# Head of a four-layer graph network on one core: ScalarE normalizes x and copies h, the attention terms come out of h's own product, and two bodies of edge ranking move beside it

## The reference, cut to what matters

```
xn  = (x - mean(x)) / sqrt(var(x) + 1e-5)
h   = xn @ W_layer.T + b_layer
a1  = (h @ w_a1.T + b_a1)[:, 0]
a2  = (h @ w_a2.T + b_a2)[:, 0]
v   = leaky_relu(a1[row] + a2[col])        # softmax of v over the edges of a row
out = segment_sum(att[:, None] * h[col], row)
```

## Time and profile before

| | us |
|---|---|
| three runs | 6016.11, 6029.7, 6051.34 |
| median | 6029.7 |
| the profiled execution | 6056.04 |
| its span | 6054.2 |
| from the statistics of x to the ranking loop | 295.25 to 396.56 |
| POOL scatters bodies 4 to 32 | 289.52 to 1113.7 |
| POOL gathers h | 1113.7 to 2166.3 |

### The profile page before, as it was taken

The page is one execution under the profiler, slowest core; times in us unless marked ns, Lnnn a source line. Parts: engine busy times, 40 slices in busy tenths (PEclk is TensorE's granted clock), DMA queues, the critical chain, the costliest instruction groups (busy, mean ns, idle before and its releaser), DMA issues.

```text
span 6054.2 us, 89560 instructions
## 1 busy us (share of the span) xinstructions
PE 4511.0 (75%) x25082; PEld 2816.0 (47%) x25082; DVE 4198.5 (69%) x9658; ACT 2286.1 (38%) x5880; POOL 4119.8 (68%) x4199
## 2 busy tenths in 40 slices
PE   6469986488888879677777767777777677777787
PEld 2135543366666646344444434444444344444455
DVE  8889986377777773676666657767676677777734
ACT  0039875355555532333333323333332232323321
POOL 1467777777777774777777757777776777777700
PEclk9579998688888879899899989999999899999989
DMA  5011110234333321544444434444444444444400
GB/s 147 19 39 29 26 27 22 72 105 109 107 101 101 102 57 39 164 135 135 128 130 130 132 104 138 137 139 138 139 139 121 133 139 138 139 138 139 138 29 21
DMA packets 445004, 624.93 MB, mean 103 GB/s; under 512 B 97098, under 2 KB 330260, under 8 KB 444563
## 3 DMA queue, kind: packets, MB, share of 16 engines
q0 software_dynamic: 187648, 457.52, 27.2%
q1 hardware_dynamic: 250164, 159.14, 9.3%
q10 hardware_dynamic: 6754, 2.96, 0.2%
HBM read 556.32 MB, written 62.94 MB: 102 GB/s over the span
## 4 chain that ended last, share of the span: by engine, by line
PE 27%; DVE 15%; issue 10%; POOL 6%; ACT 2%; DVEq 2%; DMA 2%; SPq 0%; POOLq 0%; ACTq 0%
PE banks L1169 13%; DVE acc_mem L1688 6%; POOL sort_mem L619 6%; DVE z_mem L1831 5%; PE banks L1199 4%; PE banks L1112 3%; PE banks L1102 3%; DMA sort_mem<-x_d,x_mem 2%; PE banks L1157 2%; DVEq L1677 1%; DVEq L1688 1%; ACT z_mem L805 1%; PE banks L1154 1%; ACT x_mem L816 1%; PE banks L1189 1%
## 5 line engine op out<-in xcount | busy, mean ns | idle before, releaser
L619 POOL DMA_INDIRECT sort_mem<-x_d,x_mem x2568 | 2461.9, 959 | 953.1 <-issue 831.5
L1169 PE MATMUL banks<-z_mem 128*128 128x257 f32 x5136 | 1579.8, 432 | 907.0 <-DVE acc_mem L1688 773.1
L1169 PEld LDWEIGHTS banks<-z_mem 128*128 128x128 f32 x5136 | 858.1, 200 | 1605.7 <-ACT z_mem L805 717.6
L1688 DVE TENSOR_TENSOR acc_mem<-acc_mem,banks 128x257 f32 x2568 | 1080.2, 421 | 565.2 <-PE banks L1169 391.2
L805 ACT ACTIVATE z_mem<-z_mem 128x512 f32<-128x512 f32 x1284 | 768.8, 628 | 1381.1 <-DVE z_mem L1831 1381.1
L1831 DVE TENSOR_TENSOR z_mem<-banks,sort_mem 128x512 f32<-128x512 f32 x1284 | 825.1, 685 | 411.9 <-PE banks L1157 292.8
L577 POOL DMA_INDIRECT recB_d<-acc_mem,sort_mem x740 | 787.8, 1065 | 428.1 <-issue 223.0
L586 POOL DMA_INDIRECT acc_mem<-h_d,xnt_mem x808 | 803.6, 995 | 246.3 <-issue 230.2
L1045 PE MATMUL banks<-acc_mem,xnt_mem 128*128 128x257 f32 x1616 | 577.3, 484 | 43.3 <-DVE acc_mem L1631 42.2
L1631 DVE SCALAR_TENSOR_TENSOR acc_mem<-acc_mem,z_mem,banks 128x257 f32 x808 | 386.4, 478 | 115.5 <-PE banks L1045 98.8
L1157 PE MATMUL banks<-z_mem,x_mem 32*128 32x256 f32 x5136 | 422.6, 405 | 0.0
(11 more groups left out here) (347 smaller groups left out, 5663.9 us busy)
## 6 DMA issues: line engine op xcount, KB each, us to landing
x_mem<-recB_d SPq DMA_DIRECT2D x642, 68.0 KB
sort_mem<-x_d,x_mem POOLq DMA_INDIRECT x2568
x_mem<-at_d SPq DMA_DIRECT2D x428, 64.0 KB
at_d<-x_mem SPq DMA_DIRECT2D x214, 64.0 KB
acc_mem<-h_d,xnt_mem POOLq DMA_INDIRECT x808, 2.8
x_mem<-x_d SPq DMA_DIRECT2D x100, 128.0 KB, 2.7
acc_mem<-in_edge_attr SPq DMA_DIRECT2D x40, 312.5 KB
recB_d<-acc_mem,sort_mem POOLq DMA_INDIRECT x740, 2.2
```

The costliest lines, as they stand in the source:

```text
L619: pool.indirect_dma_start(out=xg[h % XG][:, k, :], out_offset=None, in_=x_ds[l % 2], in_offset=bass.IndirectOffsetOnAxis(ap=reci[h][:, k, ...
L1169: m.matmul(bank[5 + tile % 2][:, :AC], oneh[:, Q % 2, k, :], msg[:, Q % 2, k, :], start=True, stop=True)\
L1688: v.tensor_tensor(a_, a_, bank_[:, :AC], ALU.add).then_inc(flushed, 1)
```

## The change

Edits, all in the head:

- **DVE no longer normalizes.** It computes `-mean * rs` for every tile (`norm_shift`), and ScalarE makes `xn` with one activation a tile (scale `rs`, shift `norm_shift`).
- **DVE no longer writes h.** ScalarE copies h from PSUM to `htab`, and a1's column in a second small activation.
- **Three more columns.** `wl` gets the columns D (zeros), D+1 (W times w_a2) and D+2 (W times w_a1); the products with the columns come out of the same matrix product as h. They are made once, by six multiplications with a sum (`accum_out`) on DVE.
- **One more row.** The bias `b_layer`, a 1 for column D and the folded scalar biases are a row `bias_h`; PE adds it by a product with one row of ones, first in each tile's group.
- **The loops over a1 and a2 (L1499, L1500) and the bias addition are gone.**
- **Bodies 6 and 7** are ranked in pieces between the tiles: a one-hot table at every third tile, its rank on PE a tile later, its mask and sum another tile later. The transposes use banks 6 and 7 in place of 4 and 7, since the ranks use 4 and 5.
- On ScalarE the records of body 7 come after the head's loop; before, they came ahead of it.

```diff
-        wl = z(32, 2 * D).rearrange("p (k d) -> p k d", k=2)
+        wl = z(32, 2 * (HC + 1)).rearrange("p (k d) -> p k d", k=2)
...
             sqrt_of_var(1)
+            def normalize_x(tt):
+                if tt == 0:
+                    act.wait_ge(S("head_step"), 2)
+                a.activation(xn[:, tt, :], x_sb[:, tt, :], ACT.Identity, bias=norm_shift[:, tt:tt + 1], scale=rs[:, tt:tt + 1])\
+                    .then_inc(S("xn_ready"), 1)
+            def keep_h(tt):
+                act.wait_ge(S("h_made"), tt + 1)
+                a.activation(htab[:, tt, :], bank[2 + tt % 2][:, :HC], ACT.Copy)
+                a.activation(a1[:, tt:tt + 1], bank[2 + tt % 2][:, HC:HC + 1], ACT.Copy).then_inc(S("h_read"), 1)
+            for tt in range(NT + 2):
+                if tt < NT:
+                    normalize_x(tt)
+                if tt >= 2:
+                    keep_h(tt - 2)
             make_records(RANKED_FIRST - 1)
...
+                m.matmul(bank[2 + tt % 2][:, :HC + 1], ones[0:1, :], bias_h[0:1, :], start=True, stop=False)
                 pe.wait_ge(S("xn_turn_copied"), tt + 1)
                 for k in range(2):
-                    last = m.matmul(bank[2 + tt % 2][:, :D], xtr[:, tt % 2, k * P:(k + 1) * P], wl[:, k, :],
-                                    start=(k == 0), stop=(k == 1))
+                    last = m.matmul(bank[2 + tt % 2][:, :HC + 1], xtr[:, tt % 2, k * P:(k + 1) * P], wl[:, k, :],
+                                    start=False, stop=(k == 1))
                 last.then_inc(S("h_made"), 1)
+                if tt % 3 == 1:
+                    rank_late(4 * (RANKED_FIRST - 2) + tt // 3)
             pe.wait_ge(S("h_read"), NT)
-            late_body(6)
...
-            late_body(7)
...
-            layer_norm(1, xn, "xn_ready")
-            st.did(v.memset(htab[:, :, D:D + 1], 1.0))
+            for c, col in ((1, HC), (2, D + 1)):
+                for k in range(2):
+                    st.run(v.scalar_tensor_tensor(folded, wl[:, k, :D], 1.0, vecs[:, c, :], ALU.mult, ALU.mult,
+                                                  accum_out=wl[:, k, col:col + 1]))
+                st.run(v.scalar_tensor_tensor(folded, vecs[:, 0, :], 1.0, vecs[:, c, :], ALU.mult, ALU.mult,
+                                              accum_out=bias_h[:, col:col + 1]))
+                st.run(v.tensor_tensor(bias_h[:, col:col + 1], bias_h[:, col:col + 1], small[:, 319 + c:320 + c], ALU.add))
...
+            st.run(v.scalar_tensor_tensor(norm_shift, mv[:, :, 0], -1.0, rs, ALU.mult, ALU.mult))
...
             for tt in range(NT):
-                if tt + 1 < NT:
-                    copy_turned_xn(tt + 1)
-                dve.wait_ge(S("h_made"), tt + 1)
-                v.tensor_tensor(htab[:, tt, :D], bank[2 + tt % 2][:, :D], vecs[:, 0, :], ALU.add).then_inc(S("h_read"), 1)
+                copy_turned_xn(tt)
+                g = 4 * (RANKED_FIRST - 2) + tt // 3
+                if tt % 3 == 0 and tt < 24:
+                    late_onehot(g)
+                if tt % 3 == 2:
+                    late_group(g)
             dve.wait_ge(S("h_read"), NT)
-            late_body(6)
-            for c, dst in ((1, a1), (2, a2)):
-                for t0 in range(0, NT, 5):
-                    vb = vecs[:, c:c + 1, :].broadcast_to([P, 5, D])
-                    st.run(v.tensor_tensor(dots, htab[:, t0:t0 + 5, :D], vb, ALU.mult))
-                    st.run(v.tensor_reduce(dst[:, t0:t0 + 5], dots, X_AXIS, ALU.add))
...
-            late_body(7)
```

More of the change, by code:

```diff
@@ L225, in build @@
         htab = xt_mem[:, 0:NT * HC].rearrange("p (t c) -> p t c", c=HC)
-        wl = z(32, 2 * D).rearrange("p (k d) -> p k d", k=2)
-        xtr = z(544, 2 * D).rearrange("p (h c) -> p h c", h=2)
+        wl = z(32, 2 * (HC + 1)).rearrange("p (k d) -> p k d", k=2)
+        xtr = z(552, 2 * D).rearrange("p (h c) -> p h c", h=2)
+        bias_h = z(1064, HC + 1)
+        folded = z(1324, D)
+        norm_shift = z(1580, NT)
         dots = z(1056, 5 * D).rearrange("p (t d) -> p t d", d=D)
@@ L243, in build @@
         a1 = small[:, 330:355]
-        a2 = small[:, 355:380]
         gmin = small[:, 430:432]
@@ L351, in _ @@
             sp.dma_start(x_sb[0:LAST, NT - 1, :], t["x"][(NT - 1) * P:N, :]).then_inc(S("x_loaded"), 16)
-            sp.dma_start(wl, t["W_layer_t"].rearrange("(k p) d -> p k d", p=P)).then_inc(S("att_w_loaded"), 16)
+            sp.dma_start(wl[:, :, :D], t["W_layer_t"].rearrange("(k p) d -> p k d", p=P)).then_inc(S("att_w_loaded"), 16)
             for k, name in enumerate(("L0_gnn_b_layer", "L0_gnn_w_a1", "L0_gnn_w_a2")):
@@ L957, in _ @@
             late_body(5)
-            pe.wait_ge(S("xn_ready"), 1)
-            pe.wait_ge(S("att_w_loaded"), 96)
+            pe.wait_ge(S("head_step"), 1)
             def turn_xn(tt):
+                pe.wait_ge(S("xn_ready"), tt + 1)
                 if due(tt - 1):
@@ L965, in turn_xn @@
                 for k in range(2):
-                    last = m.transpose(bank[4 + 3 * (tt % 2)][:, k * P:(k + 1) * P], xn[:, tt, k * P:(k + 1) * P], ident)
+                    last = m.transpose(bank[6 + tt % 2][:, k * P:(k + 1) * P], xn[:, tt, k * P:(k + 1) * P], ident)
                 last.then_inc(S("xn_turned"), 1)
@@ L973, in _ @@
                     pe.wait_ge(S("h_read"), tt - 1)
+                m.matmul(bank[2 + tt % 2][:, :HC + 1], ones[0:1, :], bias_h[0:1, :], start=True, stop=False)
                 pe.wait_ge(S("xn_turn_copied"), tt + 1)
                 for k in range(2):
-                    last = m.matmul(bank[2 + tt % 2][:, :D], xtr[:, tt % 2, k * P:(k + 1) * P], wl[:, k, :],
-                                    start=(k == 0), stop=(k == 1))
+                    last = m.matmul(bank[2 + tt % 2][:, :HC + 1], xtr[:, tt % 2, k * P:(k + 1) * P], wl[:, k, :],
+                                    start=False, stop=(k == 1))
                 last.then_inc(S("h_made"), 1)
+                if tt % 3 == 1:
+                    rank_late(4 * (RANKED_FIRST - 2) + tt // 3)
             pe.wait_ge(S("h_read"), NT)
-            late_body(6)
-            pe.wait_ge(S("head_step"), 1)
+            pe.wait_ge(S("head_step"), 3)
             m.transpose(bank[7][0:1, 0:P], gmin[:, 0:1], ident).then_inc(S("head_pe"), 1)
-            pe.wait_ge(S("head_step"), 2)
+            pe.wait_ge(S("head_step"), 4)
             m.matmul(bank[7][:, 256:257], ones[0:1, :], gmin[0:1, 1:2], start=True, stop=True).then_inc(S("head_pe"), 1)
@@ L986, in _ @@
             m.transpose(bank[7][:BKT_A, 0:P], a1, ident).then_inc(S("head_pe"), 1)
-            pe.wait_ge(S("head_step"), 3)
+            pe.wait_ge(S("head_step"), 5)
             for b in range(2):
@@ L1477, in _ @@
             dve.wait_ge(S("x_loaded"), 32)
-            layer_norm(1, xn, "xn_ready")
             dve.wait_ge(S("att_w_loaded"), 96)
-            st.did(v.memset(htab[:, :, D:D + 1], 1.0))
+            st.did(v.memset(wl[:, :, D:D + 1], 0.0))
+            st.did(v.tensor_copy(bias_h[:, :D], vecs[:, 0, :]))
+            st.did(v.memset(bias_h[:, D:D + 1], 1.0))
+            for c, col in ((1, HC), (2, D + 1)):
[5 more added lines that the diff above has]
+                st.run(v.tensor_tensor(bias_h[:, col:col + 1], bias_h[:, col:col + 1], small[:, 319 + c:320 + c], ALU.add))
+            dve.sem_inc(S("head_step"), 1)
+            for tt in range(NT):
+                st.did(v.bn_stats(stats[:, tt, :], x_sb[:, tt, :]))
+            st.settle()
+            for tt in range(NT):
+                st.did(v.bn_aggr(mv[:, tt, :], stats[:, tt, :]))
+            st.settle()
+            v.tensor_scalar(sd, mv[:, :, 1], EPS, None, ALU.add).then_inc(S("var_ready"), 1)
+            dve.wait_ge(S("std_ready"), 1)
+            st.run(v.reciprocal(rs, sd))
+            st.run(v.scalar_tensor_tensor(norm_shift, mv[:, :, 0], -1.0, rs, ALU.mult, ALU.mult))
+            dve.sem_inc(S("head_step"), 1)
             def copy_turned_xn(tt):
@@ L1486, in copy_turned_xn @@
                 dve.wait_ge(S("xn_turned"), tt + 1)
-                v.tensor_copy(xtr[:, tt % 2, :], bank[4 + 3 * (tt % 2)][:, :D]).then_inc(S("xn_turn_copied"), 1)
-            copy_turned_xn(0)
+                v.tensor_copy(xtr[:, tt % 2, :], bank[6 + tt % 2][:, :D]).then_inc(S("xn_turn_copied"), 1)
             for tt in range(NT):
-                if tt + 1 < NT:
-                    copy_turned_xn(tt + 1)
-                dve.wait_ge(S("h_made"), tt + 1)
-                v.tensor_tensor(htab[:, tt, :D], bank[2 + tt % 2][:, :D], vecs[:, 0, :], ALU.add).then_inc(S("h_read"), 1)
-            dve.wait_ge(S("h_read"), NT)
-            late_body(6)
-            for c, dst in ((1, a1), (2, a2)):
-                for t0 in range(0, NT, 5):
-                    vb = vecs[:, c:c + 1, :].broadcast_to([P, 5, D])
-                    st.run(v.tensor_tensor(dots, htab[:, t0:t0 + 5, :D], vb, ALU.mult))
-                    st.run(v.tensor_reduce(dst[:, t0:t0 + 5], dots, X_AXIS, ALU.add))
```

(8 more changed lines are left out.)

## The result

The changed kernel took 6059.4 us in the median (7 runs, 6043.3 to 6073.2) beside 6038.5 for the kernel before in the same rounds: ratio 1.0038, 95% interval [1.0024, 1.0052]. It is 21 us slower, where 30.6 us of gain were forecast. On another chip, eleven runs gave 1.0049 [1.0034, 1.0064]. The profiled execution after took 6073.2 us with a span of 6071.4, 17.2 us more than the span before.

The account below looks back on a forecast made before the run. POOL's unbroken run of scatters and gathers was taken to bound the kernel, once the head lets it start. Pauses 28.25 + scatters 4.9 - new holds 2.6 = 30.6 us (rounded up); 6029.7 - 30.6 = 5999.1 us, range 5981 to 6029.

Parts of the forecast that it names:

- How the head binds: Head: a microsecond saved counts only as far as POOL starts its unbroken run of scatters and gathers earlier.
- DVE ahead of the first tile: Head before the loop: six products with sums and small fills add 3.5 us; ACT's first normalization at 310.2 us.
- The loop over the tiles: Head loop: PE sets the pace at 1.59 us a tile, row of ones 0.43 of it; loop ends at 353.5 us.
- rival 3: Head loop: PE stays at 1.2 GHz, 3.18 us a tile, body 8 at 432.8, 4.5 us slower, 6034 us; chance 0.05.
- Body 8's address 30.9 us after the ranking loop's start: Start of ranking loop: body 8's addresses come 30.9 us in, as before, at 392.3 us, while POOL is at body 7.
- the store of h only as something in POOL's way: Head, beside body 6's scatters: the 3225 KB store costs POOL nothing, with 12.7 us as the bound.
- The scatters slowed by DVE: POOL's scatters in the head: 4.9 us come back without the dots, 2.6 us are lost to new work beside scatters.
- the 4.9 us: Body 6's scatters: 30.3 us beside the dots against 25.4 for bodies 4 and 5, so 4.9 us come back.
- the 2.6 us of new holds: Head scatters: 7.3 us of products and one-hot tables beside them cost 2.6 us at 0.35; bounds nothing or 7.3.
- The sum itself: Whole kernel: 30.6 us gained, body 8 at 398.1 instead of 428.26 us, median 5999.1 us; chance 0.60.
- the account of pauses: POOL in the head: the pauses before bodies 6, 7 and 8 all go, 11.92 + 15.36 + 0.97 = 28.25 us.
- the stated range: Whole kernel: 5981 us (rival 1 less the run spread) to 6029 us (rival 2 at its worst plus it), rival 3 left out.

Follow-up runs that it names:

- the early records: Changed kernel (one row, store of h first) with ACT making body 7's records behind the eighth tile instead of the last: 6077.2 us, one run.
- 128 rows: Changed kernel with the bias product over 128 equal rows, each a 128th of the bias, instead of one row: 6015.0 us, ratio 0.9962; another chip 0.9955.
- 128 rows and the rows first: Changed kernel with the bias product over 128 equal rows and body 8's row load issued before the store of h: 6001.0 us, ratio 0.9939; another chip 0.9946.
- 32 rows: Changed kernel with the bias product over 32 equal rows, each the bias divided by 32, instead of one row: 6041.1 us, one run.

## Why the prediction was wrong

*How the head binds* held. I said that a microsecond in the head counts as far as POOL starts its unbroken run earlier. The table shows that in both directions, within the spread behind it, and the early records show its other half: 5.8 us less before body 7 became 4.1 us more before body 8, which started at 451.18 us in both.

*DVE ahead of the first tile:* 3.6 us (295.22 to 298.84) for the forecast 3.5, and ACT's first normalization at 310.03 for 310.2. A product with its sum took 0.42 us and 0.08 for the read-out. A plain 256-column copy beside it took 0.39, so the half throughput that the Trainium skill ("Vector Engine (DVE) Microarchitecture Reference", Points that are easy to get wrong) gives for two such sources is not in this trace.

*The loop over the tiles* is the step that failed. I priced each pass of PE at the clock of the old loop, 1.59 us a tile, and the row of ones among them at 0.43. That sum was right at 2.4 GHz: 128 rows gave 1.59 us with a third of a rank. But with one row's product PE stayed at 1.2 GHz. The same loop came up to 2.4 GHz with 128 rows and with no product for the bias, and the loop of the kernel before, which had come up, stayed down with one such product added, so the row product is the cause. The price that failed was 1.59 us a tile for a measured 3.7: 25 tiles make 53 us, of which about 38 are the clock and 15 the few rows (an estimate from the table of tiles: 0.60 us a tile for the rows). The low clock is what rival 3 described, with a chance of 0.05 and against it the sentence that PE gets more to do in the loop. PE did get more to do, was busy 10 of 10 us, and still had 0.50. The Trainium skill ("TensorE: Matmul & The Clock Gate", Part 1: The HAM clock gate) ties the clock to how busy PE has lately been. Here kernels with PE busy 10 of 10 us stand at either level, so the busy column of these traces does not bear that out; in the pairs of one row and 128 only the rows of the product differ, beside one small operation of DVE ahead of the changed loop.

*Rival 3's price* was too low as well: 432.8 us for body 8, 6034 us, against 451.2. I had doubled the tile, a third of a rank included, to 3.18 us. That is near what 128 rows take at 0.50 (3.01 us and 0.1 for the rank); one row takes 3.71 (318.76 to 329.90 us for three). With that the loop ended at 404.2 us for the 393.2 of rival 3, 11.0 us later. What I had not seen is that a product over few rows makes itself and its neighbours dearer at the same clock. Why it does is open.

*Body 8's address 30.9 us after the ranking loop's start* failed too, by 7.3 us, in a step I had called unchanged. I took the 30.9 from a kernel in which body 7 lay between the store of h and that loop, 6.6 us in which the row load could come through (SP was held 5.44 us behind the store there too). I had named the store of h only as something in POOL's way; it stood in front of SP's next load. This was the cover that the moved body took with it. 11.0 and 7.3 make 18.3 of the 18.4 us by which rival 3 fell short.

*The scatters slowed by DVE* came out better than reckoned. Body 6, away from the dots, took 25.5 us (355.01 to 380.47, with the gap behind it), so the 4.9 us did come back. Of the 2.6 us of new holds little shows in the changed kernel: bodies 4 and 5 took 50.24 us beside the products and tables (50.44 before, counted the same way), each of the scatters beside the products took 0.96, and one beside a table took 1.17 (at 365.11 us). With 128 rows and the rows first, where more tables lie beside scatters, bodies 4 to 6 took 77.2 us (289.55 to 366.73) for the 76.2 that they would take by my sum without holds. The exclusive lock of a port pair that the Trainium skill ("SBUF — State Buffer", Who interferes with whom) describes hardly appears beside these operations. Nor does the row of 7.22 us agree with it as plainly as I wrote: the operations beside it take 0.40 us each, and the scatter stood through some eighteen of them.

*The sum itself.* With 128 rows and the rows loaded first, the ranking loop begins at 361.7 us for the forecast 361.4 and body 8 at 394.3 for 398.1, 34.0 us earlier than before, and the times are 38.6 and 33.7 us lower for the forecast 30.6. The 3.8 us are the holds (1.0 for 2.6) and body 7, which took 27.6 us for the 29.8 that I had kept from before. So the account of pauses was right, and two of its inputs were not: the price of a tile and the time to body 8's address. This version has the lowest time measured here. The ends of the stated range lie 2 and 3 us further out than the sums given for them (5982.9 and 6025.6 us).

Open: why 32 rows had both clocks, why few rows make the products beside them dearer, what one row would do to a loop that begins at 1.00, and the worth of SP's order within some 5 us.

## What to carry to other kernels

A price of PE holds at the clock of the stretch from which it was read; where a change adds a product over few rows to each step of a loop, look at the granted clock of the new loop first, check it against the length of a known row, and try the same product over all rows (equal rows, scaled down), which took the same passes and was 45 to 58 us faster here. When work is moved away, ask what it covered in every queue: here a 3.2 MB store and a small load behind it on SP. And of several pauses of one engine, what is saved in an earlier one may only move into a later one: here 5.8 us less became 4.1 us more.

## What the runs showed of the hardware that was not expected

- A loop with PE busy 10 of 10 us stayed at 0.50 of the clock for over 90 us with a product of one row in each tile (1x259 or 1x256, f32), and was granted 1.00 from 320 us on with the same product over 128 rows. 32 rows gave 0.50 for some 40 us and then 1.00 (one run).
- At one and the same clock a product over few rows made a tile dearer than the same product over 128 rows: 1.93 us for 1.54 at 1.00 (32 rows), 3.61 for 3.01 at 0.50 (one row). The clock alone made the tile 1.95 times as long (128 rows).
- PE waited 3.2 to 6.9 us for a small load that SP issued behind a 3225 KB store, in the seven profiles of the changed head with that order, and not at all in the four with the load first. SP itself was held 6.1 us at the DMA next behind the store in the changed kernel, for 0.27 us with the load first.
- In three profiles the column of the granted clock stood at 1.00 over tiles whose rows were as long as at 0.50.
